# Token routing of two FFN passes: token sums of two batches issued side by side, and a new order of the engines' work

## The reference, cut to what matters

```
x = x + 0.5 * ffn(layernorm(x))
x = x + attention(layernorm(x))
x = x + 0.5 * ffn(layernorm(x))
```

```
h = gelu(concat(x, slot_mean) @ w1 + b1)                 # per token, 128 numbers
route_logits = (h @ w2 + b2) / (abs(tau) + 0.1)          # 64 slots
topk_vals, topk_idx = top_k(route_logits, 8)
alpha = one_hot(topk_idx) weighted by softmax(topk_vals) # 64 weights per token, 8 not zero
slot_input = einsum('bts,btd->bsd', alpha, x)            # sums over the tokens
denom = alpha.sum(axis=1) + 1e-08
si = slot_input / denom
```

## Time and profile before

| | us |
|---|---|
| median of 3 runs (lowest, highest) | 3696.81 (3692.55, 3702.72) |
| the profiled execution | 3694.9 |
| its span, first to last instruction | 3692.8 |
| routing of the first ffn | 17.77 to 241.87 |
| routing of the second ffn | 3321.91 to 3545.98 |

### The profile page before, as it was taken

The page is one execution under the profiler, slowest core; times in us unless marked ns, Lnnn a source line. Parts: engine busy times, 40 slices in busy tenths (PEclk is TensorE's granted clock), DMA queues, the critical chain, the costliest instruction groups (busy, mean ns, idle before and its releaser), DMA issues. The chain is left out here.

```text
span 3692.8 us, 60507 instructions
## 1 busy us (share of the span) xinstructions
PE 3432.8 (93%) x22538; PEld 1211.2 (33%) x22538; DVE 3085.3 (84%) x4512; ACT 2729.3 (74%) x5316; POOL 932.9 (25%) x819
## 2 busy tenths in 40 slices
PE   6998489999999999999999999999999999958987
PEld 4654222232322223232323232323232322214653
DVE  6965499989899999989898989898989999807965
ACT  4740158888888888888888888888888888856730
POOL 2320311323232313232323222232323231122310
PEclk8999679999999999999999999999999999988999
DMA  3225311121212121212121211212121212112227
GB/s 102 92 93 222 119 30 42 42 54 42 57 41 73 29 68 31 70 42 53 42 62 45 54 50 45 54 42 53 42 54 42 64 40 56 34 41 92 84 78 296
DMA packets 123092, 246.53 MB, mean 67 GB/s; under 512 B 34656, under 2 KB 75424, under 8 KB 108464
## 3 DMA queue, kind: packets, MB, share of 16 engines
q1 hardware_dynamic: 115712, 208.06, 20.0%
q10 hardware_dynamic: 7088, 34.61, 2.3%
HBM read 121.91 MB, written 51.38 MB: 47 GB/s over the span
## 5 line engine op out<-in xcount | busy, mean ns | idle before, releaser
L1354 DVE TENSOR_REDUCE attn_part_max<-attn_ps 128x2 f32<-128x1024 f32 x2048 | 2447.7, 1221 | 271.1 <-PE attn_ps L1490 230.0
L1615 ACT ACTIVATE attn_probs<-attn_ps 128x512 f32<-128x512 f32 x4096 | 2177.5, 600 | 402.3 <-PE attn_ps L1502 402.1
L1502 PE MATMUL attn_ps<-attn_q_rows,attn_k_rows 50*128 50x512 f16 x4096 | 1274.8, 385 | 30.1 <-ACT attn_probs L1615 19.2
L1490 PE MATMUL attn_ps<-attn_k_rows,attn_q_rows 48*128 48x512 f16 x4096 | 1136.3, 389 | 67.8 <-DVE attn_part_max L1354 63.0
L1516 PE MATMUL attn_ps<-attn_probs,attn_v_ones 128*32 128x512 f32 x8192 | 1096.6, 607 | 0.7 <-ACT attn_probs L1615 0.7
L1502 PEld LDWEIGHTS attn_ps<-attn_q_rows,attn_k_rows 50*128 50x128 f16 x4096 | 308.2, 94 | 1310.1 <-ACT attn_probs L1615 1225.0
L1490 PEld LDWEIGHTS attn_ps<-attn_k_rows,attn_q_rows 48*128 48x128 f16 x4096 | 226.3, 94 | 226.9 <-DVE attn_part_max L1354 208.8
L1266 POOL TENSOR_TENSOR attn_xn_t<-attn_o_packed,attn_inv_wide 128x1024 f32<-128x1024 f32 x32 | 75.5, 2358 | 764.1 <-DMA attn_inv_wide<-inverse_denominators 726.0
L1516 PEld LDWEIGHTS attn_ps<-attn_probs,attn_v_ones 128*32 128x32 f32 x8192 | 161.4, 108 | 247.6 <-issue 127.2
L1442 PE MATMUL attn_ps<-attn_xn_parts,attn_w_qk 128*128 128x256 f16 x1536 | 214.6, 278 | 5.9 <-POOL attn_xn_parts L1278 5.9
L1442 PEld LDWEIGHTS attn_ps<-attn_xn_parts,attn_w_qk 128*128 128x128 f16 x1536 | 132.1, 99 | 124.4 <-issue 104.4
(11 more groups left out here) (171 smaller groups left out, 2661.2 us busy)
## 6 DMA issues: line engine op xcount, KB each, us to landing
attn_q_rows<-attn_parts SPq DMA_DIRECT2D x384, 64.0 KB, 2.3
attn_k_rows<-attn_parts SPq DMA_DIRECT2D x384, 64.0 KB, 2.3
ffn_x_ring<-in_L_attn_x SPq DMA_DIRECT2D x16, 1024.0 KB, 5.8
attn_x_ln<-after_first_ffn SPq DMA_DIRECT2D x16, 1024.0 KB, 5.2
attn_o_packed<-attn_o_sb SPq DMA_DIRECT2D x256, 64.0 KB, 2.3
attn_inv_wide<-inverse_denominators SPq DMA_DIRECT2D x32, 512.0 KB
attn_x_res<-after_first_ffn SPq DMA_DIRECT2D x16, 1024.0 KB, 5.1
after_attention<-attn_x_res SPq DMA_DIRECT2D x16, 1024.0 KB, 8.6
```

The source lines that it names most:

```text
L1354: dve.tensor_reduce(part_max[:, G % 2, :, j, t, half], pair, AX.X, ALU.max).then_inc(dve_emptied, 1)
L1490: last = pe.matmul(ps[:, bank + e, :], q_rows[rows_e, G % NG, j, t * P:(t + 1) * P], k_rows[rows_e, G % NG, j, half * HALF:(half + 1) * HA ...
L1502: pe.matmul(ps[:, bank, :], k_rows[rows_e, G % NG, h // 2, kt * P:(kt + 1) * P], q_rows[rows_e, G % NG, h // 2, half * HALF:(half + 1) * H ...
L1615: act.activation(probs[:, quad % NQ, h, :], bank_of(s, b0), ACT.Exp, scale=1.0 / (SCALE * SCALE)).then_inc(act_emptied, 1)
```

## The change

The ring has 8 places. The step order is new: `normalise` works two batches ahead and `statistics` three, `rstd`, `shift` and `mean_var` have two places, and the loop has 21 steps. The sums of a pair are issued together, tile by tile, with the two halves in turn; half of the tiles in an odd step n (pair (n-3)/2), the other half in the next. DVE gives `neg_mean`, and POOL makes `shift` right after the power. `less_largest` also subtracts within the eight largest, Exp takes 576 columns in place of 512, and the total is the sum over those 8 in place of all 64 picked ones. The loads wait for the sums of the pair that had the place before.

```diff
     TT = T // P
     NS = B * S
     PAIRS = B // 2
-    R = 4
+    R = 8
     def rows(t, b):
...
+                for b in range(B):
+                    if b >= R:
+                        sp.wait_ge(si_ready, (b - R) // 2 + 1)
+                    sp.dma_start(x_ring[:, b % R, :, 0:D], rows(x_in, b)).then_inc(x_loaded[b % R], 16)
...
+                    if b >= 2:
+                        pool.wait_ge(xn_low, b - 1)
+                        pool.wait_ge(xn_high, b - 1)
+                    pool.tensor_tensor(rstd[:, b % 2, :], var_eps[:, :], c.neg_half[:, 0:TT], ALU.pow).then_inc(rstd_ready, 1)
+                    pool.wait_ge(rstd_ready, b + 1)
+                    pool.tensor_tensor(shift[:, b % 2, :], neg_mean[:, :], rstd[:, b % 2, :], ALU.mult).then_inc(shift_set, 1)
...
+                    if b >= 1:
+                        pool.wait_ge(exp_done, b)
+                    pool.tensor_tensor(shifted[:, :, 0:S], logit[:, :, :], top8[:, :, 0:1].to_broadcast([P, TT, S]),
...
-                def scale(b, pair, r, n):
+                    pool.tensor_tensor(shifted[:, :, S:S + 8], top8[:, :, :], top8[:, :, 0:1].to_broadcast([P, TT, 8]),
+                                       ALU.subtract).then_inc(shift_ready, 1)
...
+                    if pair >= 2:
                         pool.wait_ge(at_ready, pair - 1)
-                    pool.tensor_tensor(alpha[:, r // 2, :, r % 2, :], picked[:, :, :],
+                        pool.wait_ge(si_ready, pair - 1)
...
+                rsqrt(1)
+                rsqrt(2)
+                for n in range(B):
+                    less_largest(n)
+                    if n + 3 < B:
+                        rsqrt(n + 3)
+                    scale(n)
...
+                    if b >= 1:
+                        dve.wait_ge(shift_set, b)
...
+                    dve.tensor_scalar(neg_mean[:, :], mean_var[:, b % 2, :, 0], -1.0, None, ALU.mult)
+                    dve.tensor_scalar(var_eps[:, :], mean_var[:, b % 2, :, 1], EPS, None, ALU.add).then_inc(var_ready, 1)
...
+                    dve.tensor_reduce(total[:, :], expd[:, :, S:S + 8], AX.X, ALU.add).then_inc(pick_step, 1)
+                    dve.scalar_tensor_tensor(picked[:, :, :], rest[:, :, :], NEG, expd[:, :, 0:S], ALU.is_equal,
                                              ALU.mult).then_inc(pick_step, 1)
                     dve.wait_ge(pick_step, b * 3 + 1)
-                    dve.tensor_reduce(total[:, :], picked[:, :, :], AX.X, ALU.add).then_inc(pick_step, 1)
...
+                statistics(0)
+                normalise(0)
+                statistics(1)
+                normalise(1)
+                statistics(2)
+                for n in range(STEPS):
+                    if n < B:
+                        find_top(n)
+                    if n + 2 < B:
+                        normalise(n + 2)
+                    if n + 3 < B:
+                        statistics(n + 3)
+                    if n < B:
+                        weigh(n)
+                    if n % 2 == 0 and 4 <= n <= B + 2:
+                        divide((n - 4) // 2)
...
+                def sum_tokens(pair, tiles):
                     if tiles[0] == 0:
-                        pe.wait_ge(alpha_ready, b + 1)
-                        if n >= 2 and e == 0:
+                        pe.wait_ge(alpha_ready, 2 * pair + 2)
+                        if pair >= 1:
                             pe.wait_ge(si_taken, pair)
                     for t in tiles:
-                        last = pe.matmul(ps_si[e * S:(e + 1) * S, 0:D + 1], alpha[:, r // 2, t, e, :], x_ring[:, r, t, :],
-                                         start=(t == 0), stop=(t == TT - 1), skip_group_check=True)
+                        for e in range(2):
+                            last = pe.matmul(ps_si[e * S:(e + 1) * S, 0:D + 1], alpha[:, pair % 2, t, e, :], x_ring[:, (2 * pair + e) % R, t, :],
+                                             start=(t == 0), stop=(t == TT - 1), skip_group_check=True)
...
+                turn_rows(0, (0, 1, 2, 3))
+                for n in range(STEPS):
+                    pair, first = (n - 3) // 2, 0 if n % 2 else TT // 2
+                    summing = 0 <= pair < PAIRS
                     if n < B:
-                        turn_rows(b, r, n, (0, 1))
-                    sums(0)
+                        hidden(n)
+                    if n + 1 < B:
+                        turn_rows(n + 1, (0, 1))
                     if n < B:
-                        turn_rows(b, r, n, (2, 3))
-                    sums(1, 2, 3)
-                    if n < B:
-                        hidden(b, n)
-                    if n % 2 == 0 and n >= 4:
-                        turn_sums(pairs_of(q, r))
-                    sums(4, 5, 6, 7)
-                    if n % 2 and 3 <= n <= B + 1:
-                        turn_weights(pairs_of(q, r), r, n)
-                    if n < B:
-                        logits(b, n)
-                over_batches(pe, step)
+                        logits(n)
+                    if n + 1 < B:
+                        turn_rows(n + 1, (2, 3))
+                    if n % 2 and 5 <= n <= B + 3:
+                        turn_sums((n - 5) // 2)
+                    if summing:
+                        sum_tokens(pair, range(first, first + TT // 2))
+                    if n % 2 and summing:
+                        turn_weights(pair)
...
+                def weights(b):
+                    act.wait_ge(shift_ready, 2 * b + 2)
+                    if b >= 1:
+                        act.wait_ge(pick_step, 3 * (b - 1) + 2)
+                    act.activation(expd[:, :, :], shifted[:, :, :], ACT.Exp).then_inc(exp_done, 1)
...
+                normalise(0)
+                take_rows(0, (0, 1, 2, 3))
+                normalise(1)
+                for n in range(STEPS):
+                    if 1 <= n <= B:
+                        weights(n - 1)
                     if n < B:
...
+                        take_rows(n + 1, (0, 1))
+                    if n + 2 < B:
+                        normalise(n + 2)
+                    if n + 1 < B:
+                        take_rows(n + 1, (2, 3))
+                    if n % 2 and 5 <= n <= B + 3:
+                        pair = (n - 5) // 2
+                        act.wait_ge(si_turned, pair + 1)
+                        act.activation(si_t[:, :, pair * P:(pair + 1) * P],
                                        ps_at[:, 0, 0:D].rearrange("p (k s) -> p k s", k=KT),
                                        ACT.Identity).then_inc(si_t_ready, 1)
-                over_batches(act, step)
+                    if n % 2 and 3 <= n <= B + 1:
+                        pair = (n - 3) // 2
+                        act.wait_ge(at_ready, pair + 1)
```

160 lines of the change are left out of this document (52 added, 108 removed).

## The result

| | before | after |
|---|---|---|
| median of 5 runs, us | 3696.81 | 3672.78 |
| lowest to highest, us | 3692.55 to 3702.72 | 3672.09 to 3674.76 |
| profiled execution, us (span) | 3694.9 (3692.8) | 3672.18 (3670.4) |
| first routing, stage start to slot products, us | 224.10 | 208.79 |
| second routing, us | 224.07 | 213.78 |

The changed kernel is faster by 0.6%: ratio 0.9937, 95% interval 0.9922 to 0.9951, or 24.0 us. The forecast was 3663 us, 33.8 less, range 3645 to 3684: the direction and the range held, and the saving was 0.71 of the one forecast. The prediction's narrower range of 3655 to 3672 was missed by 0.8 us. Executions of one and the same kernel can differ by some 20 us: the kernel before took 3686 to 3703 in most and 3711 to 3716 in some, at a mean granted clock of 0.966 to 0.973 and of 0.962 to 0.963, so a median of few executions is uncertain by several us.

The account below looks back on a forecast made before the run. The prediction took TensorE as the bound, VectorE close behind. Each routing saves 18.5 us less 1.7 for the clock: 3694.9 - 2 x (18.5 - 1.7) = 3661.3 us profiled; the median lies 1.9 above, 3663, range 3645 to 3684.

Parts of the forecast that it names:

- TensorE set the pace, and pairing relieves it: Steady part: TensorE busy 24.25 of 24.49 us per pair; with paired sums the pair falls to 21.95.
- the attention's rows: Four f32 matmuls on four column places take 1.00 us, one 0.91; taken to give 0.49 us for two sums.
- the Trainium skill's three-tile figure: 2.38 times for three column tiles; as an estimate, two sums at 0.58 us and a result about 6 us later.
- The even step: Logits to logits on TensorE: logits 1.7, transposes 1.1, sums 2.0 and 4.9 more, 9.7 us in all.
- VectorE and GpSimd stay below: VectorE needs 19.9 us per pair, leaving 2; GpSimd gets 0.25 for the shift and is far from full.
- ScalarE in the odd step: Weights' copy, table loads and Exp take 4.3 us ahead of gelu; with the shift path the odd step is 12.25.
- the sum of 3661.3: Forecast for the profiled execution: 3694.9 us less, in each of two routings, 18.5 saved minus 1.7 for the clock.
- the tails: End of each routing, from the 16th logits to the slot stage: 18.9 us.
- The clock's charge of 3.4: One more fall of TensorE's clock per routing, while there are no sums: 1.7 us charged for each.
- TensorE alone: Rival, chance 0.17: TensorE alone sets the pace, pairs of 20.9 us and the clock holds, 3649 us.
- Held instructions of VectorE: Rival, chance 0.12: normalising and `picked` each held 0.87 us per step beside GpSimd; 23.4 per pair, 3679 us.
- Serial halves: Rival, chance 0.06: the halves don't run side by side; a step's sums take 3.7 us, pair 25.1, 3710 us.

Follow-up runs that it names:

- Experiment 11: Kernel before, old step order and unpaired sums, with only the shift's product on GpSimd and the total from the eight largest: 3696.59 us, ratio 0.9997.
- 1: Changed kernel with ScalarE's copy of the turned sums moved ahead of the normalising in odd steps: 3663.87 us, ratio 0.9923.
- 5: Changed kernel with the statistics four batches ahead instead of three, three buffers for mean, power and shift, ten ring places: 3660.23 us, ratio 0.9901.
- experiment 3: Changed kernel with each step's four left-half matmuls issued first, then the four right-half ones, not in turn: 3694.21 us, ratio 0.9997.
- 4: Kernel before in its old step order, with paired sums on the two halves, ring of eight, division one step later, sums' transposes moved: 3704.17 us, ratio 1.0020.
- experiment 9: Changed kernel with statistics four batches ahead and the turned weights' copy behind the next even step's gelu: 3649.73 us, ratio 0.9870.
- 12: Kernel before, old order, with paired sums, shift's product on GpSimd, total from the eight largest, and sums' transposes just ahead of hidden: 3688.12 us, ratio 0.9971.

## Why the prediction was right, and where it was off

**TensorE set the pace, and pairing relieves it: right in the main.** Experiment 11, without pairing, had a pair 0.3 us shorter and both routings 7.4 us shorter behind the first logits, so VectorE had a small share in the old pace. Eight paired sums take 1.96 us (forecast 2.0), so two cost 0.49 as the attention's rows said. Two serial sums cost 0.92. By the Trainium skill's three-tile figure (TensorE: Matmul & The Clock Gate, section Part 3: Packing small matmuls — row/col tiling), as an estimate, eight would have taken 2.3; the trace does not agree, it has 1.96. The even step came out at 9.61 (9.7).

**VectorE and GpSimd stay below: right.** GpSimd's product takes 0.20 (0.25), the 64 extra columns 0.29, the variance comes 8.3 after find_top as forecast, and no small instruction of VectorE is stretched to 1.00 any more. VectorE waits 3.46 us per pair, where I expected 1 to 2.

**ScalarE in the odd step: here the prediction failed.** It said 12.25, and 13.34 was measured. The failing words are "the weights' copy, with the small copy of the sums ahead of it, slips to 6.8". I let the copy of the sums (0.37 us) only delay the next copy on ScalarE. I did not ask who waits for it on TensorE: `turn_weights`, by the order of the two uses of `ps_at`. The chain has 1.1 us more by that: the weights' copy started 7.85 us after the logits (118.40 to 126.25) and not 6.8. After the row copies come the sums' copy and then TensorE's 1.1 of transposes, where I had these transposes long done. Experiments 1 and 5 show it from both sides. The five pairs of a routing together came 5.0 us late, in both routings; that is 10 of the 10.9 us that the profiled execution stands above the sum of 3661.3.

**The rest of the sum.** The setup ended 2.8 us later than before; its code is the same, and experiments 3 and 4 had it at the old speed, so this isn't the change. From the stage's start to the fifth logits it took 65.3 and 68.6 us for the 67.2 forecast; the last step of the second routing 11.2 for 9.7, the tails 19.2 each for 18.9. The attention between took 1.0 longer, and what lies behind the second routing and around the span 0.9 less. The clock's charge of 3.4 was in the sum as a term of its own, and what the clock really cost is contained in these. Together 2.8 - 2.0 + 1.4 + 1.5 + 0.5 + 1.0 - 0.9 - 3.4 = 0.9, which with the pairs' 10.0 is the 10.9.

**The clock: right in kind, wrong in place.** The 1.7 was charged behind the start's gap in both routings. In the first the clock held there (1.00 from 54 to 62 us); in the second it fell behind a wait of 4.30 us (last row). At the end of the first it fell behind one of 3.11, where eight sums took 2.69 us for 1.96 and the granted clock was 0.79 from 220 to 228:

```profile
220.34 0.41 PE L496 MATMUL ffn_ps_at<-ident,ffn_si_rows 128*128 128x128 f32 x2 [3.11 <-DVE ffn_si_rows L420]
220.68 2.69 PE L479 MATMUL ffn_ps_si<-ffn_x_ring,ffn_alpha 128*64 128x257 f32 x16
...
3350.31 6.11 PE L459 MATMUL ffn_ps_hid<-ffn_xn_t,w 128*128 128x512 f32 x8 [4.30 <-ACT ffn_xn_t L533]
```

Hidden takes 3.60 to 3.70 at full clock. Windows of 8 us from 3342 and from 3350 have a granted clock of 0.90 and 0.68, so it stood at the lower level of 1.2 GHz for part of both.

**The rivals.** TensorE alone at 20.7 to 20.9 per pair did not happen in the changed kernel, but experiment 9 went below it (20.37) once the waits were gone. Held instructions of VectorE were not seen. Serial halves were forced by experiment 3 and gave no gain rather than the loss forecast. The forecast had 25.1 per pair; the usual pair was 22.99 and the mean 23.64, since serial halves still overlap in part (2.88 for 3.7) and the loop had slack in the odd step. The rival's own sum had slips as well: 7.8 + 0.2 + 4.3 + 1.17 is 13.5 and not 13.7, so its pair was 24.9, and its limit for two sums is 0.80 and not 0.78.

## What to carry to other kernels

When two uses share a PSUM space, the copy that frees it belongs as early in its engine's order as its input allows: ask of every small copy who waits for it on the other engines, not only what stands behind it on its own. When no engine is full and the period stays the same although single steps vary, add up the loop through the engines; any of its links, the cheapest to move first, is a place to cut it. And cutting the load of the bounding engine pays only as far as the work around it is ready earlier as well: here pairing without the deeper order made the median 6 us shorter at best and 15 longer at worst. And read a change of one stage from the rows of that stage: experiments 3, 11 and 12 look different there than by the median.
